# The last stage of an audio tower kernel with another layout of the output: 64 consecutive tokens on each partition, weights stacked high over low, two products a mix, and the output sums shared with GpSimd

## Chip, cores and metric

The kernel runs on one core of a Trainium2 chip. The metric is device time in microseconds (us) of one execution, lower is better. TensorE is called PE in the profile's rows, VectorE DVE, ScalarE ACT, GpSimd POOL, SyncE SP.

## What is computed

The input x is 64 sequences of 125 steps with 128 features. Three parts follow one another:

```python
h = _L0_tok_ref(x, L0_tok_kernel)                      # window-3 convolution to 3x128, tanh / sigmoid gates, recurrence over t
h = h + _L0_attn_ref(_layernorm(h), A, B, h0)           # long convolution per channel, gelu
h = h + _L0_ffn_ref(_layernorm(h), gate_weight, w1, w2) # 16 experts, top 2 per token
```

The last part is what matters here. Every one of the 64 x 123 = 7872 tokens picks 2 of 16 experts; each expert's hidden vectors are averaged over its tokens, and one output vector per expert is made of the mean. A token's result is a mix of two of the 16 output vectors:

```python
h = silu(einsum('td,efd->tef', x, w1))
h_sum = einsum('tef,te->ef', h, mask); h_mean = h_sum / max(counts, 1)
y_mean = einsum('ef,edf->ed', h_mean, w2)
out = einsum('tk,tkd->td', routing_w, y_mean[top_idx])
```

## The kernel before

The residual H lies in SBUF as 123 partitions (t) by 64 sequences (b) by 128 features. `build` writes one instruction stream per engine (`@block.sync` for SP, `@block.gpsimd`, `@block.tensor`, `@block.scalar`, `@block.vector`), ordered by hand; semaphores join them, and each engine runs its own stream in order.

**The expert stage.** GpSimd gathers 138 tiles of 128 tokens from the DRAM array `table` (`gather`, L613-617), 3 to a group. The first 60 tiles have places of their own in XN; from then on 24 places (8 groups) are used in turn, and GpSimd waits for TensorE's `group_mm` before it overwrites a group (L624). For each group TensorE transposes 3 tiles (L899), ScalarE copies them out (L1248), then TensorE multiplies each with its expert's w1 (L929), ScalarE does silu in PSUM (L1259) and VectorE adds the tile to the expert's sum (L1706). Six PSUM banks go round, so TensorE waits for the add of tile n-6. 60 tiles are written out, 72 are a loop, 6 are written out again (L1039-1047). On SP the load of w2 stands behind a wait for TensorE's 20th group (L522-523).

**The picks' matrix.** At tiles 16 and 17 VectorE makes L, 123 x 64 x 16: for each token the weights of its two picks at their experts' places (L1782, L1784), and sets `R_ready`. It is needed transposed, with 8 sequences x 16 experts = 128 rows. This is done in two rounds, at tiles 23 and 26 (`RT_AT`): TensorE makes 4 transposes into bank P[5] (L1019), ScalarE rounds them to the high part (L1272), VectorE subtracts for the low part (L1791).

**The end.** Expert sums go through a product with ones (L1056, or as high and low part L1062 and L1063 with a cast by ScalarE, L1325, and a subtraction by GpSimd, L637), and VectorE reduces each over w2 (L1807) to y. Two transposes (L1067) bring y in rows; ScalarE copies it 8 times under the mask `bmask`, one sequence's 16 rows each (L1330), and VectorE makes the 8 low parts (L1815). Then come 16 mixes of 4 sequences: three products each (high x high, low x high, high x low, L1081) in one of 4 banks, an add into H by VectorE (L1822), and a store of H to `out` (L437), the even ones by SP, the odd by ScalarE. Such a store has 123 x 4 pieces of 512 bytes, since tokens of one t and neighbouring b lie 123 x 128 numbers apart in `out`. Every store is cut into 112 partitions and 11 (`SPLIT`).

## Time and profile before

| | |
|---|---|
| median of 3 runs | 514.2 us (513.64 to 516.24) |
| the profiled execution | 512.89 us |
| its span in the trace | 511.1 us |
| busy, share of the span | PE 78%, DVE 61%, ACT 43%, POOL 40% |
| DMA | 43.68 MB in 53020 packets, 85 GB/s on the mean |
| TensorE's granted clock | 0.867 of full speed |

The profile is of one execution. Engine shares are means over stages with different limits, so they do not name the bound of any one stage; the stretches and timelines in the section on rows do. "PEld" is TensorE's loading of weights. In rows of a timeline the bracket at the end gives the engine's idle time before the instruction and what ended it; "issue" there means that it waited for nothing that the profile shows.

### The profile page before, as it was taken

The numbers are of one execution on the slowest core, as the hardware profiler recorded it, in microseconds if no ns is written. First come the engines' busy times: TensorE is split into PE (matmuls) and PEld (weight loads), VectorE is DVE, ScalarE is ACT, GpSimd is POOL, SyncE is SP. The second block draws the span as 40 slices with busy tenths as digits, with TensorE's granted clock in tenths as the row PEclk, the third lists the DMA queues.
The fourth block names the chain that finished last, engine by engine and source line by source line (L and its number), as shares of the span: only waits on it lengthen the run. The fifth ranks groups of instructions, "written<-read, shape, count | busy, mean of one in ns | idle before, by whom it ended". The sixth has DMA issues, their size and how long they took to land.

```text
span 511.1 us, 7309 instructions
## 1 busy us (share of the span) xinstructions
PE 399.0 (78%) x1929; PEld 268.5 (53%) x1930; DVE 311.2 (61%) x827; ACT 217.9 (43%) x423; POOL 205.0 (40%) x231
## 2 busy tenths in 40 slices
PE   8999999998998987240458414589979796899983
PEld 7888888887998964120344101244434242344562
DVE  3598888889788999600354111477744453467894
ACT  3334555554233766320536101456644463457320
POOL 2011101116202998776055776400066665610510
PEclk9999999998998996755668756699997987989997
DMA  7207433322219330922341122100191111100039
GB/s 180 64 1 183 127 101 87 90 79 81 80 34 292 85 80 14 291 52 51 126 153 43 53 53 55 26 5 2 50 327 46 47 41 41 46 10 1 1 78 240
DMA packets 53020, 43.68 MB, mean 85 GB/s; under 512 B 20686, under 2 KB 45980, under 8 KB 52732
## 3 DMA queue, kind: packets, MB, share of 16 engines
q1 hardware_dynamic: 44276, 32.09, 21.9%
q0 software_dynamic: 4416, 9.05, 6.7%
q10 hardware_dynamic: 4296, 2.15, 1.6%
q8 instruction: 15, 0.25, 0.2%
q14 instruction: 17, 0.14, 0.1%
HBM read 34.86 MB, written 8.42 MB: 85 GB/s over the span
## 4 chain that ended last, share of the span: by engine, by line
PE 47%; another core or an unknown queue 16%; DVE 15%; ACT 8%; issue 7%; POOL 3%; DVEq 2%; ACTq 0%; POOLq 0%
PE P L656 18%; PE P L929 13%; PE P L861 5%; ACT P L1259 4%; DVE BIG L1706 3%; DVE H L1822 2%; PE P L899 2%; PE P L1056 2%; PE P L649 2%; PE P L682 1%; POOL XN L597 1%; ACT XN L1180 1%; DVE arena L1498 1%; POOL arena L594 1%
## 5 line engine op out<-in xcount | busy, mean ns | idle before, releaser
L929 PE MATMUL P<-w1T,arena 128*128 x276 | 144.8, 657 | 23.3 <-DVE BIG L1706 14.9
L1706 DVE TENSOR_TENSOR BIG<-BIG,P 128x512 f32 x138 | 94.9, 688 | 103.9 <-issue 57.9
L929 PEld LDWEIGHTS P<-w1T,arena 128*128 128x128 f32 x276 | 51.7, 208 | 79.1 <-issue 78.7
L614 POOL DMA_INDIRECT XN<-table,arena x60 | 58.0, 967 | 39.2 <-issue 18.5
L1259 ACT ACTIVATE P<-P 128x512 f32<-128x512 f32 x138 | 72.8, 580 | 1.6 <-PE P L929 1.5
L1248 ACT COPY arena<-P 128x384 f32<-128x384 f32 (+1 forms) x48 | 22.4, 466 | 110.6 <-remote 63.3
L614 POOL DMA_INDIRECT arena<-table,arena x42 | 39.6, 944 | 60.9 <-PE P L929 44.1
L557 POOL TENSOR_TENSOR rs<-ve,mhalf 123x4 f32<-123x4 f32 x16 | 17.5, 1096 | 101.9 <-DVE ve L1350 101.9
L1097 ACT ACTIVATE arena<-P 128x492 f32<-128x492 f32 x48 | 27.9, 583 | 50.4 <-PE P L656 50.4
L614 POOL DMA_INDIRECT BIG<-table,arena x36 | 34.5, 958 | 22.3 <-remote 10.4
L656 PE MATMUL P<-xh,wh 128*128 128x498 f32 x144 | 42.3, 402 | 0.0
L656 PE MATMUL P<-xh,wl 128*128 128x498 f32 x144 | 40.5, 390 | 0.0
L656 PE MATMUL P<-xl,wh 128*128 128x498 f32 x144 | 40.4, 389 | 0.0
L656 PEld LDWEIGHTS P<-xl,wh 128*128 128x128 f32 x144 | 27.2, 189 | 5.6
L656 PEld LDWEIGHTS P<-xh,wl 128*128 128x128 f32 x144 | 27.1, 188 | 5.4
L861 PE MATMUL P<-XN,BIG 123*123 123x112 f32 (+1 forms) x256 | 27.7, 271 | 1.2 <-DVE XN L1395 1.2
L656 PEld LDWEIGHTS P<-xh,wh 128*128 128x128 f32 x144 | 26.2, 192 | 4.1
L861 PEld LDWEIGHTS P<-XN,BIG 123*123 123x123 f32 x256 | 27.6, 188 | 1.4 <-DVE XN L1395 1.4
L594 POOL TENSOR_TENSOR arena<-arena,mhalf 123x16 f32<-123x16 f32 x4 | 11.7, 2925 | 31.6 <-DVE arena L1514 31.6
L899 PE MATMUL P<-ident,XN 128*128 128x128 f32 x60 | 11.0, 296 | 16.7 <-issue 10.1
L597 POOL TENSOR_SCALAR XN<-H,arena 123x128 f32<-123x128 f32 x24 | 23.3, 985 | 0.3
L899 PEld LDWEIGHTS P<-ident,XN 128*128 128x128 f32 x60 | 8.0, 152 | 27.4 <-issue 27.4
(242 smaller groups left out, 637.9 us busy)
## 6 DMA issues: line engine op xcount, KB each, us to landing
arena<-kpad SPq DMA_DIRECT2D x16, 492.0 KB, 4.0
XN<-in_L_ffn_w SPq DMA_DIRECT2D x1, 4096.0 KB
arena<-in_x SPq DMA_DIRECT2D x16, 224.0 KB
table<-XN SPq DMA_DIRECT2D x4, 896.0 KB
BIG<-table SPq DMA_DIRECT2D x1, 2048.0 KB
out<-H SPq DMA_DIRECT2D x8, 224.0 KB
out<-H ACTq DMA_DIRECT2D x8, 224.0 KB
BIG<-table SPq DMA_DIRECT2D x1, 1024.0 KB
```

Of the source, the lines that this page charges most:

```text
L557: nc.gpsimd.tensor_tensor(rs1[0:T, k], ve1[0:T, k], mhalf[0:T, 0:CB], ALU.pow).then_inc(rstd1, 1)
L594: nc.gpsimd.tensor_tensor(rs2[0:T, qb], ve2[0:T, qb], mhalf[0:T], ALU.pow).then_inc(rstd2, 1)
L597: a = nc.gpsimd.tensor_scalar(XN[0:T, b], H[0:T, b], mm2[0:T, 0, b:b + 1], rs2[0:T, b:b + 1], ALU.subtract, ALU.mult)
L614: pool.indirect_dma_start(out=row_of(n), out_offset=None, in_=table[0:(QA * QB + 1) * TROW, :] if n < NA else table[:, :], in_offset=bass. ...
L656: mm = nc.tensor.matmul(PG[g][:, 0:NV], wpart[:, w, g * D:(g + 1) * D], xpart[:, k, w:w + NV], start=(place == 0 and w == 0), stop=(place ...
L861: mm = nc.tensor.matmul(PG[g % 3][0:T, j * B:j * B + n], hank[0:T, c // HP % HRES, c % HP], XF[0:T, c * B:c * B + n], start=True, stop=True)
L899: mm = nc.tensor.transpose(PT[:, j * SLOT:(j + 1) * SLOT], src, ident[:])
L929: mm = nc.tensor.matmul(bank[:, :], stat, w1T[:, bass.ds(e * FF, FF)], start=True, stop=True)
L1097: nc.scalar.activation(dst[:, k].rearrange("p (b t) -> p b t", b=CB), src, func).then_inc(gate_act, 1)
L1248: nc.scalar.copy(GTs[:, bank, 0:count * SLOT], PT[:, 0:count * SLOT]).then_inc(GT_ready, 1)
L1259: nc.scalar.activation(bank[:, :], bank[:, :], ACT.Silu).then_inc(silu_done, 1)
L1706: v.tensor_tensor(at, at, bank[:, :], ALU.add).then_inc(esum_step, 1)
```

## The change

1. **Layout of the last stage.** After the norms have read H for the last time, SP writes H to `out` as it is (512-byte pieces) and reads it back so that partition p holds the 64 consecutive tokens 64p to 64p+63 (4 KB pieces). At the end a store of 4 tokens per partition is one piece of 2 KB (`ov`).
2. **The picks' matrix takes the same trip.** L goes to `out` in pieces of 64 bytes and comes back twice in pieces of 256 bytes, side by side (`twice`): 4 tokens x 16 experts, and the same 64 numbers again.
3. **Transposes of it.** 4 rounds in place of 2. Rounds 0 and 1 stand among the last six tiles, rounds 2 and 3 behind them; nothing is left at tiles 23 and 26. A transposed tile has the weights in rows 0 to 63 and again in 64 to 127; ScalarE rounds all 128 rows, VectorE makes the low part in rows 64 to 127 alone.
4. **Two products a mix.** (high over low) x high of y with 128 rows, and high x low of y with 64 rows. y is copied for 4 tokens in place of 8; GpSimd folds `bmask` for it at the start. The mixes have 6 banks in place of 4.
5. **Sums.** Of the 16 sums GpSimd makes numbers 2, 5, 8, 11, 14, each after a copy from PSUM by ScalarE; VectorE makes the other 11.
6. 3 warming products in place of 8 stand before the expert sums' products.

```diff
@@ layout, names, sharing
+        twice = R2.rearrange("p k b e -> p (k b e)").rearrange("p (n m) -> p n m", n=NCH)
-        RTh, RTl = (a[:, :, 0:4 * T].rearrange("p h (g t) -> p h g t", g=4) for a in (xh, xl))
-        yh, yl = (a[:].rearrange("p w n -> p (w n)")[:, 0:HB * D].rearrange("p (b d) -> p b d", b=HB) for a in (wh, wl))
+        RT = [a[:, h, 0:4 * T] for a in (xh, xl) for h in range(2)]
+        yh, yl = (a[:].rearrange("p w n -> p (w n)")[:, 0:CB * D].rearrange("p (b d) -> p b d", b=CB) for a in (wh, wl))
-        PRT = P[5]
+        PRT = (P[5], P[5], P[5], P[4])
+        MIX = (P[0], P[1], P[2], P[3], P[6], P[7])
-        RT_AT = (23, 26)
+        RT_ROUNDS = 4
+        ADD_POOL = list(range(2, 2 * NHB, 3))
+        ADD_DVE = [n for n in range(2 * NHB) if n not in ADD_POOL]
-        ov = out.rearrange("b t d -> t b d")
+        ov = out.rearrange("b t d -> (b t d)").rearrange("(p r d) -> p r d", p=T, r=B)
@@ SP
             clear(15, 6, 8)
+            by_t = out.rearrange("b t d -> t b d")
+            for g in range(NQ):
+                for lo, hi in ((0, SPLIT), (SPLIT, T)):
+                    sp.dma_start(by_t[lo:hi, g * QB:(g + 1) * QB], H[lo:hi, g * QB:(g + 1) * QB]).then_inc(H_out, 16)
+            sp.wait_ge(H_out, 2 * NQ * 16)
+            for r in range(0, B, HB):
+                for lo, hi in ((0, SPLIT), (SPLIT, T)):
+                    sp.dma_start(H[lo:hi, r:r + HB], ov[lo:hi, r:r + HB]).then_inc(H_in, 16)
+            sp.wait_ge(H_in, 2 * NHB * 16)
+            sp.wait_ge(R_ready, 1)
+            sp.dma_start(bass.AP(out.tensor, 0, [[E, T], [T * E, B], [1, E]]), L[0:T]).then_inc(R_out, 16)
+            sp.wait_ge(R_out, 16)
+            for k in range(2):
+                sp.dma_start(twice.rearrange("p n (k m) -> p n k m", k=2)[0:T, :, k],
+                             bass.AP(out.tensor, 0, [[B * E, T], [CB * E, NCH], [1, CB * E]])).then_inc(R_in, 16)
             sp.wait_ge(group_mm, EARLY_GROUPS)
@@ GpSimd
+            nc.gpsimd.tensor_tensor(bmask[:, 0:CB], bmask[:, 0:CB], bmask[:, CB:HB], ALU.add)
...
+            pool.wait_ge(H_in, 2 * NHB * 16)
+            for i, n in enumerate(ADD_POOL):
+                pool.wait_ge(mix_copied, i + 1)
+                hv = H[0:T, 4 * n:4 * (n + 1)].rearrange("p b c -> p (b c)")
+                nc.gpsimd.tensor_tensor(hv, junk[i % 2][0:T], hv, ALU.add).then_inc(mixed_pool, 1)
@@ TensorE
+            def weights(h):
+
+                if h == 0:
+                    pe.wait_ge(R_in, 32)
+                elif h < 3:
+                    pe.wait_ge(RT_low, h)
+                for k in range(4):
+                    mm = nc.tensor.transpose(PRT[h][:, k * T:(k + 1) * T], twice[0:T, 4 * h + k], ident[0:T, 0:T])
+                mm.then_inc(RT_mm, 1)
...
-            keep_warm(PT, 8)
+            weights(2)
+            weights(3)
+            pe.wait_ge(esum_step, NT - REGS + 1)
+            keep_warm(P[0], 3)
...
             for n in range(2 * NHB):
...
+                at = slice(n % 4 * T, (n % 4 + 1) * T)
+                nc.tensor.matmul(MIX[n % len(MIX)][0:T, :], RT[n // 4][:, at], yh.rearrange("p b d -> p (b d)"),
+                                 start=True, stop=False)
+                if n == 0:
+                    pe.wait_ge(yl_ready, 1)
+                nc.tensor.matmul(MIX[n % len(MIX)][0:T, :], RT[n // 4][0:64, at], yl[0:64].rearrange("p b d -> p (b d)"),
+                                 start=False, stop=True).then_inc(mix_mm, 1)
@@ ScalarE
+            def high_weights(h):
+                act.wait_ge(RT_mm, h + 1)
+                nc.scalar.copy(RT[h], PRT[h][:, 0:4 * T]).then_inc(RT_high, 1)
...
+                if n in (NT - REGS, NT - REGS + 2):
+                    high_weights((n - NT + REGS) // 2)
+            high_weights(2)
+            high_weights(3)
...
+            stores = list(range(1, 2 * NHB, 2))
+            for i, n in enumerate(ADD_POOL):
+                act.wait_ge(mix_mm, n + 1)
+                if i >= 2:
+                    act.wait_ge(mixed_pool, i - 1)
+                nc.scalar.copy(junk[i % 2][0:T], MIX[n % len(MIX)][0:T, :]).then_inc(mix_copied, 1)
+                store(act, stores[i])
+            for n in stores[len(ADD_POOL):]:
                 store(act, n)
@@ VectorE
+            def low_weights(h):
+                dve.wait_ge(RT_high, h + 1)
+                low = RT[h][64:128]
+                v.tensor_tensor(low, PRT[h][64:128, 0:4 * T], low.bitcast(FP32), ALU.subtract).then_inc(RT_low, 1)
+
             for n in range(NT - REGS, NT):
                 add_tile(n)
+                if n in (NT - REGS, NT - REGS + 2):
+                    low_weights((n - NT + REGS) // 2)
+            low_weights(2)
+            low_weights(3)
...
+            dve.wait_ge(H_in, 2 * NHB * 16)
+            for n in ADD_DVE:
                 dve.wait_ge(mix_mm, n + 1)
```

The order on TensorE at the last six tiles, before. `P<-w1T,arena` is a tile's product, `P<-ident,arena 128x128` the transpose of the next tile:

```order
L899 MATMUL P<-ident,arena 128x128
L929 REGISTER_ALU x2
L929 ISA
L929 MATMUL P<-w1T,arena 128x512
L929 REGISTER_ALU x2
L929 ISA
L929 MATMUL P<-w1T,arena 128x512
L899 MATMUL P<-ident,arena 128x128
L929 REGISTER_ALU x2
L929 ISA
L929 MATMUL P<-w1T,arena 128x512
```

And in the changed kernel, from the same transpose on (L943 is the old L899, L973 the old L929, L1075 are the picks' transposes of `weights`):

```order
L943 MATMUL P<-ident,arena 128x128
L1075 MATMUL P<-ident,arena 128x123 x4
L973 REGISTER_ALU x2
L973 ISA
L973 MATMUL P<-w1T,arena 128x512
L973 REGISTER_ALU x2
L973 ISA
L973 MATMUL P<-w1T,arena 128x512
L943 MATMUL P<-ident,arena 128x128
L1075 MATMUL P<-ident,arena 128x123 x4
L973 REGISTER_ALU x2
L973 ISA
```

Round 0 comes ahead of the second and third of the six tiles, round 1 ahead of the fourth.

ScalarE in the last stage, changed kernel (L1383 is the copy of a mix for GpSimd, L458 a store in its two parts):

```order
L1377 ACTIVATE wh<-P,bmask 128x128 x4
L1383 COPY arena<-P 123x512
L458 DMA out<-H 112x512
L458 DMA out<-H 11x512
L1383 COPY arena<-P 123x512
L458 DMA out<-H 112x512
L458 DMA out<-H 11x512
```

Copies and odd stores alternate five times, then three more stores follow; before, eight masked copies were followed by eight stores.

## Rows read from the trace of the kernel before

**Rows 1.** The page's chain of work that ended last: shares by engine.
```profile
PE 47%; another core or an unknown queue 16%; DVE 15%; ACT 8%; issue 7%; POOL 3%; DVEq 2%; ACTq 0%; POOLq 0%
```

**Rows 2.** Stretches: start:end, length, busy us (count) by engine, clock, DMA share, GB/s.
```profile
core 0: us, PE busy (x) PEld busy (x) DVE busy (x) ACT busy (x) POOL busy (x), PEclk, DMA share, GB/s
283.00:325.00 42.00, 12.55 (x21) 3.74 (x20) 4.81 (x7) 4.58 (x10) 27.28 (x30) 0.59 0.18 46
...
340.00:370.00 30.00, 30.00 (x94) 14.64 (x93) 20.49 (x31) 19.95 (x42) 0.00 (x0) 1.00 0.06 14
370.00:452.00 82.00, 67.48 (x172) 29.68 (x171) 39.83 (x58) 36.99 (x77) 50.02 (x53) 0.88 0.28 89
```

**Rows 3.** Timeline of VectorE at the last tiles and the first reduction.
```profile
471.23 5.61 DVE L1706 TENSOR_TENSOR BIG<-BIG,P 128x512 f32 x7 [0.22 <-DVE BIG L1706]
478.16 0.69 DVE L1807 CUSTOM_DVE_ANT_0 arena<-XN,P 128x512 f32<-128x512 f32 x1 [1.33 <-PE P L1056]
```

**Rows 4.** Timeline, last stage: start, length, instruction, count, idle before and its releaser.
```profile
490.38 2.18 ACT L1330 ACTIVATE wh<-P,bmask 128x128 fp32r<-128x128 f32 x8 [3.80 <-PE P L1067]
490.86 2.16 DVE L1815 SCALAR_TENSOR_TENSOR wl<-P,bmask,wh 128x128 fp32r<-128x128 f32 x8 [1.00 <-ACT wh L1330]
...
492.93 11.13 DVE L1822 TENSOR_TENSOR H<-P,H 123x512 f32<-123x512 f32 x16
...
493.64 13.57 SPq L437 DMA_DIRECT2D out<-H  x16
```

**Rows 5.** Stretches, DMA alone: start:end, length, clock, DMA share, GB/s.
```profile
494.00:509.00 15.00, 0.88 0.99 259
369.00:381.00 12.00, 1.00 1.03 374
...
500.00:502.00 2.00, 1.00 1.04 271
...
508.00:510.00 2.00, 0.50 0.83 227
510.00:512.00 2.00, 0.50 0.01 3
```

**Rows 6.** Groups by line and shape, 476 to 490 us: busy us, mean ns.
```profile
L637 POOL TENSOR_TENSOR wl<-BIG,wh 128x512 fp32r<-128x512 f32 x7 | 8.9, 1278 | 25.9 <-ACT wh L1325 25.8
L1325 ACT CAST wh<-BIG 128x512 fp32r<-128x512 f32 x7 | 4.2, 617 | 7.1 <-PE P L1063 5.5 <-DVE BIG L1706 1.6
```

**Rows 7.** Timeline at tiles 23 and 26: the two rounds of picks' transposes.
```profile
333.73 0.46 PEld L1019 LDWEIGHTS P<-ident,arena 123*128 123x128 f32 x4 [0.56 <-DVE arena L1784]
333.83 0.59 PE L1019 MATMUL P<-ident,arena 123*128 123x123 f32 x4
...
337.05 0.58 ACT L1272 CAST xh<-P 128x492 fp32r<-128x492 f32 x1
...
338.29 0.66 DVE L1791 TENSOR_TENSOR xl<-P,xh 128x492 fp32r<-128x492 f32 x1
...
339.10 0.61 PE L1019 MATMUL P<-ident,arena 123*128 123x123 f32 x4 [1.69 <-DVE xl L1791]
...
339.55 0.49 PE L899 MATMUL P<-ident,XN 128*128 128x128 f32 x3
```

**Rows 8.** Waits of SP's queue: us in total, times, longest us.
```profile
SPq L523 <- PE P L929: 101.8, 1, 101.8
```

**Rows 9.** Timeline of GpSimd: end of the long train of gathers, and the next.
```profile
317.42 0.94 POOL L614 DMA_INDIRECT BIG<-table,arena  x1 [0.31 <-issue]
324.55 0.94 POOL L614 DMA_INDIRECT BIG<-table,arena  x1 [6.19 <-remote]
```

**Rows 10.** DMA issues: queue, count, KB each, median us from issue to landing.
```profile
arena<-kpad SPq DMA_DIRECT2D x16, 492.0 KB, 4.0
...
kpad<-H ACTq DMA_DIRECT2D x1, 128.0 KB, 1.7
```

**Rows 11.** Timeline of TensorE: six passes of three tiles, twice.
```profile
437.75 2.74 PE L929 MATMUL P<-w1T,arena 128*128 x6
...
445.87 4.75 PE L929 MATMUL P<-w1T,arena 128*128 x6
```

More of the change, by code:

```diff
@@ L400, in build @@
         R_ready = sem("R_ready")
+        R_out = sem("R_out")
+        R_in = sem("R_in")
+        H_out = sem("H_out")
+        H_in = sem("H_in")
         RT_mm = sem("RT_mm")
@@ L429, in hankel @@
             return bass.AP(kpad.tensor, q * HP * KROW, [[1, 128], [KROW, HP], [1, T]])
[L431 removed]
+        ov = out.rearrange("b t d -> (b t d)").rearrange("(p r d) -> p r d", p=T, r=B)
         def store(queue, n):
[L435 removed]
+            queue.wait_ge(*added(n))
             for lo, hi in ((0, SPLIT), (SPLIT, T)):
@@ L1008, in _ @@
                 expert_of(n)
-                if n in RT_AT:
-                    pe.wait_ge(R_ready, 1)
-                    h = RT_AT.index(n)
-                    if h == 0:
-                        pe.wait_ge(ring_read, MATCH_AT[NQ - 1, PER_Q - 1] + 1)
-                    else:
-                        pe.wait_ge(RT_low, h)
-                    for k in range(4):
-                        b = (4 * h + k) * HB
-                        mm = nc.tensor.transpose(PRT[:, k * T:(k + 1) * T],
-                                                 L[0:T, b:b + HB].rearrange("p b e -> p (b e)"), ident[0:T, 0:T])
-                    mm.then_inc(RT_mm, 1)
             with pe.Fori(0, PASSES) as i:
@@ L1036, in _ @@
                                group_mm if k == 0 else None)
-            nc.tensor.matmul(PRT[:, 0:128], onef[:], onef[:], start=True, stop=True).then_inc(last_mm, 1)
+            def weights(h):
[6 more added lines that the diff above has]
+                mm.then_inc(RT_mm, 1)
+            nc.tensor.matmul(PRT[0][:, 0:128], onef[:], onef[:], start=True, stop=True).then_inc(last_mm, 1)
             expert_of(NT - REGS)
             transposes_of(TRIPLES + 1)
+            weights(0)
             expert_of(NT - REGS + 1)
@@ L1043, in _ @@
             transposes_of(TRIPLES + 2)
+            weights(1)
             expert_of(NT - 3)
@@ L1328, in _ @@
             act.wait_ge(y_transposed, 1)
-            for b in range(HB):
+            for b in range(CB):
                 nc.scalar.mul(yh[:, b], P[4][:, 0:128], bmask[:, b:b + 1]).then_inc(yh_ready, 1)
-            for n in range(1, 2 * NHB, 2):
+            stores = list(range(1, 2 * NHB, 2))
[6 more added lines that the diff above has]
+            for n in stores[len(ADD_POOL):]:
                 store(act, n)
@@ L1812, in _ @@
             dve.wait_ge(y_transposed, 1)
[L1813 removed]
+            for b in range(CB):
                 dve.wait_ge(yh_ready, b + 1)
[L1815 to L1819 removed]
+                a = v.scalar_tensor_tensor(out=yl[0:64, b], in0=P[5][0:64, 0:128], scalar=bmask[0:64, b:b + 1],
+                                           in1=yh[0:64, b].bitcast(FP32), op0=ALU.mult, op1=ALU.subtract)
+            a.then_inc(yl_ready, 1)
+            dve.wait_ge(H_in, 2 * NHB * 16)
+            for n in ADD_DVE:
                 dve.wait_ge(mix_mm, n + 1)
                 hv = H[0:T, 4 * n:4 * (n + 1)].rearrange("p b c -> p (b c)")
[L1822 removed]
+                v.tensor_tensor(hv, MIX[n % len(MIX)][0:T, :], hv, ALU.add).then_inc(mixed, 1)
 _INS = ["x", "L0_tok_kernel", "L0_attn_A", "L0_attn_B", "L0_attn_h0", "L0_ffn_gate_weight", "L0_ffn_w1", "L0_ffn_w2"]
```

44 lines of the change are left out of this document (13 added, 31 removed).

## The prediction

> **What bounds the kernel now.** I read the shares of the chain first [rows 1]: TensorE has 47% of it, so no single engine is the bound everywhere; the stages must be taken apart. The table by stretches [rows 2] does that: look at how much of a stretch each engine is busy. Two kinds of stretches matter here. From 340 to 370 us TensorE is busy 30.0 of 30 us: anything taken off TensorE in front of it is taken off the end. From 283 to 325 and from 370 to 452 us no engine is full; there GpSimd issues gathers and the others crawl.
>
> The last stretches are the object of the change. From 467 on the adds of the last tiles run back to back on VectorE, 7 of them in 5.61 us, and the first reduction over w2 starts 1.3 us after the last add [rows 3]. At 490.4 the picks' matrix is built, then VectorE makes the 16 output sums in 11.13 us without a gap [rows 4]: TensorE's 48 products do not hold it up. But VectorE is not the end either. It is through at 504.06; the span goes on to 511.1, and there is still DMA at a share of 0.83 from 508 to 510. From the first store on, all DMA engines are full, at 259 GB/s on the mean and 271 in a full stretch [rows 5]. So the end is set by writing 4.03 MB (123 x 64 rows of 512 bytes) in pieces of 512 bytes, from 493.6 (end of the first add) to about 510.2, 16.6 us.
>
> **The tail.** With 64 tokens in a row on a partition, a store of 4 tokens is one piece of 2 KB per partition. No row shows such a write. The nearest on one side is the same write in 512-byte pieces, 259 to 271 GB/s; on the other the load of w2, also 2 KB pieces and also with all engines full, but reading HBM: 374 GB/s with some gathers in it [rows 5]. I take 374, because both cases have a share of 1.0 and differ mainly in bytes per piece. 4.03 MB / 374 GB/s = 10.8 us.
>
> The Trainium skill, in "DMA: Bandwidth & Descriptors", section Specifications, says that 512 bytes is the smallest transfer at line rate, by which 2 KB pieces would write no faster. The trace disagrees as far as reads go [rows 5]; no row shows the write, so this stays a rival, below.
>
> Can the sums feed this? VectorE now makes 11 at 0.69 us = 7.6 us. GpSimd makes 5: a two-input 128x512 operation took it 1278 ns, and ScalarE's copy of 512 columns before each is some 617 ns [rows 6]. Counted from the first product (sum n ready = 0): VectorE's sums 0, 1, 3, 4 are done at 0.7, 1.4, 2.1, 2.8, GpSimd's 2, 5, 8, 11, 14 at about 3.3, 4.6, 5.9, 7.2, 8.5. SP stores the even sums in order, so it holds 4 and 6 behind sum 2; ScalarE stores the odd ones and its later copies queue behind the wait for sum 5 (4.6). Three stores go out early, then the queue idles about 0.5 us until 3.3, and from there the other 13 follow each other at 0.67 us. The end comes at about 13.1, or 12.4 after the first add against 16.6 now: **-4.2 us**.
>
> Ahead of it, ScalarE makes 4 masked copies of y instead of 8 and VectorE 4 low parts instead of 8, 0.27 us each [rows 4]. Eight low parts now end at 493.02, where the first add could start; four end at about 491.95, then comes the second product, so the first add starts at 492.4: **-0.5 us**.
>
> **The weights' transposes, taken out at tiles 23 and 26.** TensorE waited 0.56 us for VectorE's sum of the picks and did four transposes (about 0.45 more until its next work); at tile 26 it sat idle 1.69 us until VectorE, which was behind by the picks' multiplications, had made the low part, then four transposes again [rows 7]. Together 0.56 + 0.45 + 1.69 + 0.45 = 3.15. Without them TensorE runs a little into the wait for its banks, so I take **-2.7 us**; bounds 0 and 3.15. This is in front of the full 30 us of TensorE [rows 2], and the restart of the gathers and w2's load are both tied to TensorE's progress, so what follows should move up with it.
>
> **The same work, put at the end.** Four rounds of four transposes, a cast on ScalarE (0.58 us as at L1272) and a low part on VectorE (0.66 us as at L1791) [rows 7]. Rounds 0 and 1 stand among the last six tiles, where VectorE has no gap. They cost it 2 x 0.66 = 1.3. Round 1 costs more: its transposes reuse round 0's bank and wait for VectorE's low part 0, which comes after the add of tile NT-6; behind that wait in TensorE's order are the last three tiles. Walking it through with the durations of the rows: low part 0 ends at 473.4 (this trace's time scale), transposes to 474.05, tile 135's add at 475.75, the last two tiles' adds at 477.2 and 478.1, the end at 478.8 instead of 476.84: +2.0. Low parts 2 and 3 (1.3 us) fit into the 1.32 us before the first reduction [rows 3]. ScalarE's last two casts end about 0.45 us after the last add and push its first cast of an expert's sum by as much: +0.4. **+2.4 us**, bounds 1.3 (VectorE's work alone) and 3.5.
>
> **The two trips through `out`.** SP writes H (4 MB, 512-byte pieces) and reads it back in 4 KB pieces, from 265 us on. At the rates of [rows 5] that is 15 + 11 us and two latencies, over by about 295. SP has nothing else: its next wait, for w2, lasts 101.8 us [rows 8]. Gathers share the DMA engines, but they are needed 20 us and more later, and GpSimd's pace of one per 1.25 us decides that stage: its train of gathers ends at 317.42 and the next comes at 324.55 [rows 9]. It costs nothing as long as that pace holds. The second trip, of the picks' matrix, starts when R_ready is set (333.7) and must be back when TensorE reaches round 0 of the transposes, at 469.4 - 2.7 = 466.7: 133 us of cover. The extra GpSimd add at the start stands beside TensorE's warm-up: nothing.
>
> **Sum.** -4.2 - 0.5 - 2.7 + 2.4 = -5.0. The profiled execution took 512.9 us (span 511.1), so 507.9 on its scale. It was 1.3 us under the median of the runs (514.2), so the forecast is **509.2 us**, 1.0% faster.
>
> **Rivals.**
>
> *The small pieces come back too late (slower).* R_out has 123 x 64 = 7872 pieces of 64 bytes, R_in 3936 of 256. Spread over 16 engines that is 738 per engine; over three it is 3936. The nearest rows: 1024 pieces of 492 bytes landed in 4.0 us, a 128-piece write in 1.7 [rows 10], so (4.0 - 1.7) / 64 = 36 ns a piece; a full stretch of the 512-byte write gives 30 (512 bytes at a 16th of 271 GB/s) [rows 5]. Sixteen engines need 27 us. Three need 3936 x 36 + 3.4 = 145 us, 12 more than the cover: 521 us. It decides from 33 ns a piece; 64-byte pieces should be cheaper than that. Against 16 engines speaks that each other transfer of 123 rows in this kernel is cut in 112 and 11, and these three are not. 11%.
>
> The same page of the Trainium skill ("Why a DMA increments its semaphore by 16 and not by 1") says that a DMA uses the largest number of engines up to 16 that divides its outermost count; for 123 this is 3. No row here shows it.
>
> *2 KB pieces write no faster than 512-byte ones.* The engines are full in the tail already, and if a piece costs by its bytes the write stays at 16.6 us: -0.5 - 2.7 + 2.4 = -0.8, 513.4 us. Against it stands the 374 of [rows 5]. 8%.
>
> That is what the rule of the Trainium skill's "DMA: Bandwidth & Descriptors" quoted above would give.
>
> *The middle keeps the 2.7 us.* Between 370 and 452 us gather trains and slow stretches follow each other, and TensorE is busy only 67 of 82 us [rows 2]; a stage that waits on itself can swallow a shift. 511.9 us. 14%.
>
> *GpSimd's sums are slow beside VectorE's.* At twice 1278 ns five take 12.8 us, the last store comes near 16: 512.1 us. Against it: the reduction beside L637 takes its 0.69 us at 478.16 as others do [rows 3]. 6%.
>
> *TensorE's clock falls while it waits for round 1 and for the last add.* After an idle stretch at 443 us six passes took 4.75 us instead of 2.74 [rows 11]; twice that price on the sums' products gives +4, 513.2 us. 8%.
>
> **How the numbers follow.** The forecast keeps 53%; its own range is 507.1 (end +1.3, middle -3.15, tail 0.6 better) to 511.5. About 0.5%, 2.6 us, is what a measurement of this kernel can tell from no change: the bounds are 511.6 and 516.8. Faster: the forecast's 53%, half of the middle rival, and 4 of the 22% of the three rivals behind it, whose prices are upper ones: 49 + 7 + 4 = 0.60 (4 of the 53 fall within). Within: 4 + 7 + 14 of the 22 = 0.25. Slower: the late trip, and 4 where two of the others meet: 0.15. The range for 8 in 10 reaches from 505.5 (the forecast's low end, and the scatter of the runs shown, 2.6 us, once more in part) to 515.5, over the rivals but the late trip.
>
> **What would show it.** Last stretch: DMA share 1.0 at 350 GB/s or more, last packet some 12.4 us after the first add; if under 290 GB/s, the tail is wrong. At tiles 23 and 26 no idle time of TensorE. VectorE's last tile add about 2 us later, relative to the last gather, with four 64x492 operations. GpSimd's five sums near 1.3 us. R_in landed before 466. If w2's load or TensorE's first `weights` waits on DMA, the forecast is wrong by that wait.

## The result and the profile after

The changed kernel is slower: 520.38 us (median of 4 runs, 518.10 to 521.75) against 513.92 us. The ratio is 1.0121, 95% interval 1.0086 to 1.0156. The forecast was 509.2 us, 505.5 to 515.5.

The two profiled executions are 519.14 us (span 517.4) and 512.89 us (span 511.1), so there are 6.3 us to explain. The later runs fell on chips of two kinds: on chips 4 and 12 the kernel before takes 512 to 515 us, as in the first measurement; on chips 1 and 2 it takes 421 us. Times are therefore compared as ratios to the kernel before on the same chip.

The page of the changed kernel has this line to set beside [rows 1] (shares by engine of the chain of work that ended last):

```profile
PE 50%; another core or an unknown queue 15%; DVE 11%; ACT 9%; issue 8%; POOL 3%; DVEq 1%; POOLq 0%; ACTq 0%
```

The entry POOLq (GpSimd's queue) has 0%, there as here, and looks like nothing, but here it is the last link. This is the end of the chain of the changed kernel in order of time (start, length, what):

```profile
503.52 0.59 ACT arena L1383
504.12 0.07 issue
504.19 1.30 POOL H L682
505.48 1.20 issue
506.69 1.32 POOLq L140
```

The span ends at 517.4, on GpSimd's queue, and on an instruction of L140, the line of the block that frames the whole program. The record calls it a DRAIN, the instruction with which GpSimd ends its stream; it ends at 517.17, when nothing else runs; the kernel before ended its chain in VectorE's sums. The stretches of the changed kernel say so (columns as in [rows 2]):

```profile
494.00:500.00 6.00, 6.00 (x15) 2.52 (x14) 3.45 (x5) 1.17 (x2) 2.17 (x2) 1.00 0.48 146
500.00:506.00 6.00, 6.00 (x16) 2.57 (x15) 3.46 (x6) 1.17 (x2) 3.00 (x3) 1.00 0.80 259
506.00:512.00 6.00, 0.86 (x3) 0.31 (x2) 0.69 (x1) 0.59 (x1) 1.28 (x1) 0.60 0.82 266
...
513.00:517.00 4.00, 0.00 (x0) 0.00 (x0) 0.00 (x0) 0.00 (x0) 0.00 (x0) 0.50 0.00 0
```

Two things are to be seen. First, four whole microseconds without an engine and without DMA. Second, the DMA share in the tail is 0.48 and 0.80, where it was 0.99 in [rows 5]: the writes no longer set the pace, they wait for sums and, as shown below, for their issue. The timeline shows for whom the sums wait (start, length, instruction, idle time before it and its releaser):

```profile
494.14 0.18 PEld L1123 LDWEIGHTS P<-wh,xh 128*123 128x123 f32 x1 [0.24 <-issue]
494.14 0.49 PE L1123 MATMUL P<-wh,xh 128*123 128x512 f32 x1
494.32 1.46 DVE L1878 TENSOR_TENSOR H<-P,H 123x512 f32<-123x512 f32 x2 [0.65 <-PE P L1127]
494.56 0.18 PEld L1127 LDWEIGHTS P<-wl,xh 64*123 64x123 f32 x1 [0.24 <-issue]
494.56 0.49 PE L1127 MATMUL P<-wl,xh 64*123 64x512 f32 x1
494.97 0.18 PEld L1123 LDWEIGHTS P<-wh,xh 128*123 128x123 f32 x1 [0.24 <-issue]
...
496.77 0.69 DVE L1878 TENSOR_TENSOR H<-P,H 123x512 f32<-123x512 f32 x1 [1.00 <-PE P L1127]
...
506.72 1.28 POOL L682 TENSOR_TENSOR H<-arena,H 123x512 f32<-123x512 f32 x1 [1.24 <-ACT arena L1383]
506.90 0.69 DVE L1878 TENSOR_TENSOR H<-P,H 123x512 f32<-123x512 f32 x1 [0.99 <-PE P L1127]
```

Weight loads start every 0.42 us, and each has 0.24 us of idle time before it. A busy PE (6.00 of 6) hides this: MATMUL spans are drawn so that they touch. In the kernel before the loads of the same stage follow each other every 0.23 us with no idle time:

```profile
495.04 0.18 PEld L1081 LDWEIGHTS P<-wl,xh 128*123 128x123 f32 x1
495.27 0.18 PEld L1081 LDWEIGHTS P<-wh,xh 128*123 128x123 f32 x1
495.50 0.18 PEld L1081 LDWEIGHTS P<-wh,xl 128*123 128x123 f32 x1
```

So 32 products at 0.42 us (13.5 us) replaced 48 at 0.23 us (11.2 us): fewer products, more time. VectorE waits about 1 us for TensorE ahead of five of its eleven sums, those that follow a mix left to GpSimd.

An idle time before a load proves nothing by itself. The tile products of the kernel before have 128 rows each time, and their loads too stand 0.42 us apart with 0.24 us before each:

```profile
434.84 2.74 PE L929 MATMUL P<-w1T,arena 128*128 x6
435.28 0.19 PEld L929 LDWEIGHTS P<-w1T,arena 128*128 128x128 f32 x1 [0.24 <-issue]
435.70 0.19 PEld L929 LDWEIGHTS P<-w1T,arena 128*128 128x128 f32 x1 [0.24 <-issue]
```

Those operands are declared as plain fp32, those of the mixes as fp32r (`xh`, `xl`, `wh`, `wl`), so the comparison that counts is between mixes of the two kernels.

ScalarE holds stores back as well. Its queue has a copy and an odd store in turn, and a store that is ready waits for the copy in front of it:

```profile
503.52 0.58 ACT L1383 COPY arena<-P 123x512 f32<-123x512 f32 x1 [1.95 <-PE P L1127]
503.53 0.79 ACTq L458 DMA_DIRECT2D out<-H  x2
506.07 4.06 ACTq L458 DMA_DIRECT2D out<-H  x8
```

The stores at 503.53 and 506.07 are those of mixes 7 and 9, whose sums ended at 500.84 and 502.52: 2.7 and 3.5 us late. In the run without sums on GpSimd (a1, below) every odd store goes 0.03 to 0.04 us after its sum.

Where the 6.3 us are, from the records of the two traces (start or end in us of the span; the profiles of two experiments beside them):

| | before | changed | a1 | a3 |
|---|---|---|---|---|
| 131st tile add starts | 470.32 | 469.97 | 470.50 | 469.26 |
| last tile add starts | 476.14 | 477.82 | 479.52 | 478.28 |
| first output sum starts | 492.93 | 494.32 | 496.00 | 494.77 |
| last sum ends | 504.06 | 508.00 | 509.29 | 504.43 |
| last packet of a store ends | 510.27 | 512.44 | 512.26 | 510.10 |
| DRAIN of GpSimd (L140) ends | 497.11 | 517.17 | 500.49 | 499.24 |
| span | 511.1 | 517.4 | 513.2 | 511.2 |

Column by column, changed less before: up to the 131st tile -0.35; the last tiles +2.0; expert sums and the low parts of y -0.3; from the first sum to the last packet +0.8; from the last packet to the end +4.1. That makes +6.3. These are single profiles: the 131st tile scatters by 2.2 us between profiles, and in the kernel before the stretch from the first sum to the last packet is 16.8 us in another profile (b1).

### The profile page after: what moved, and what is told of

Same layout as the page of the kernel before. It is cut to its first block, busy times and chain, and to the rows that moved or that the text cites. A ratio compares the mean times of both kernels' runs of the same rounds, so it can differ in the third digit from the quotient of the medians.

```text
span 517.4 us, 7306 instructions
## 1 busy us (share of the span) xinstructions
PE 399.2 (77%) x1911; PEld 265.0 (51%) x1912; DVE 308.9 (60%) x820; ACT 220.7 (43%) x426; POOL 211.5 (41%) x237
## 4 chain that ended last, share of the span: by engine, by line
PE 50%; another core or an unknown queue 15%; DVE 11%; ACT 9%; issue 8%; POOL 3%; DVEq 1%; POOLq 0%; ACTq 0%
PE P L700 15%; PE P L973 14%; PE P L905 6%; ACT P L1303 5%; PE P L943 2%; PE P L735 2%; PE P L1102 2%; DVE BIG L1760 2%; PE P L693 1%; POOL XN L636 1%; ACT XN L1224 1%; DVE arena L1552 1%; PE P L823 1%; POOL arena L633 1%
## 5 line engine op out<-in xcount | busy, mean ns | idle before, releaser
L973 PE MATMUL P<-w1T,arena 128*128 x276 | 144.4, 656 | 15.6 <-DVE BIG L1760 9.5
L973 PEld LDWEIGHTS P<-w1T,arena 128*128 128x128 f32 x276 | 52.7, 210 | 71.9 <-issue 71.7
L943 PE MATMUL P<-ident,XN 128*128 128x128 f32 x60 | 11.1, 299 | 28.0 <-issue 15.0
L905 PE MATMUL P<-XN,BIG 123*123 123x112 f32 (+1 forms) x256 | 29.4, 280 | 2.6 <-DVE XN L1449 2.6
L905 PEld LDWEIGHTS P<-XN,BIG 123*123 123x123 f32 x256 | 29.2, 197 | 2.8 <-DVE XN L1449 2.8
L943 PEld LDWEIGHTS P<-ident,XN 128*128 128x128 f32 x60 | 8.3, 156 | 38.7 <-issue 38.7
```

Of the source, the lines that this page charges most:

```text
L905: mm = nc.tensor.matmul(PG[g % 3][0:T, j * B:j * B + n], hank[0:T, c // HP % HRES, c % HP], XF[0:T, c * B:c * B + n], start=True, stop=True)
L943: mm = nc.tensor.transpose(PT[:, j * SLOT:(j + 1) * SLOT], src, ident[:])
L973: mm = nc.tensor.matmul(bank[:, :], stat, w1T[:, bass.ds(e * FF, FF)], start=True, stop=True)
```

## The experiments

The theory has two parts. A: GpSimd's closing DRAIN lasts a fixed time beyond its last work, and the last sums on GpSimd brought it out from under the stores. B: the change between 128-row and 64-row weights exposes each load. The rivals are named in the expectations.

**1. No sums on GpSimd (a1).** Of the changed kernel:

```diff
-        ADD_POOL = list(range(2, 2 * NHB, 3))
+        ADD_POOL = []
```

> The changed kernel with all 16 last sums on VectorE, none on GpSimd. Theory A: GpSimd ends the program with a DRAIN that lasts 9.2 us beyond its last operation (it ends at 497.1 us in the kernel before, where GpSimd's last work ends at 487.9, and at 517.2 in the changed one, where that ends at 508.0), and this sets the end of the changed kernel. Then it ends near 499 here, and the span ends with SyncE's wait for the last store: 512.3 to 513.3 us instead of 517.4, a time of about 514.5. Rival: the DRAIN only lasts until something else is over (the last stores, the other engines), and the span stays at 517 us. TensorE's products stay at 0.42 us each in both.

Measured: 515.72 us, ratio 1.0003 (0.9969 to 1.0037); span 513.2. The DRAIN ends at 500.49 and the span at the last store. GpSimd's last operation ends at 491.33 here, 9.16 us ahead of that; in the changed kernel it is 508.00 and 517.17. A holds. From the first sum to the last packet it is 16.3 us, where the changed kernel has 18.1: the held stores of ScalarE are gone with the copies. The ratio fell by 0.0118 (6.1 us), the span by 4.2; between their intervals anything from 2.5 us on is open, so the runs ask for no second cause. The products still go at 0.42 us.

**2. 128 rows in both products (a2).** The low weights stand in rows 64 to 127 of RT, so yl over all rows only adds low times low.

```diff
-                nc.tensor.matmul(MIX[n % len(MIX)][0:T, :], RT[n // 4][0:64, at], yl[0:64].rearrange("p b d -> p (b d)"),
+                nc.tensor.matmul(MIX[n % len(MIX)][0:T, :], RT[n // 4][:, at], yl.rearrange("p b d -> p (b d)"),
...
-                a = v.scalar_tensor_tensor(out=yl[0:64, b], in0=P[5][0:64, 0:128], scalar=bmask[0:64, b:b + 1],
-                                           in1=yh[0:64, b].bitcast(FP32), op0=ALU.mult, op1=ALU.subtract)
+                a = v.scalar_tensor_tensor(out=yl[:, b], in0=P[5][:, 0:128], scalar=bmask[:, b:b + 1],
+                                           in1=yh[:, b].bitcast(FP32), op0=ALU.mult, op1=ALU.subtract)
```

> The changed kernel with the second product of each mix over all 128 rows (and yl made for all 128) instead of 64. Theory B: the change between weights of 128 and of 64 rows keeps the next load from running beside the product, so each product costs 0.42 us (load 0.18 + columns 0.23). With 128 rows in both the distance falls to 0.23 us as in the kernel before, the last sum ends near 502.5 instead of 508 us, and GpSimd's DRAIN ends near 512: span 511.8 to 513 us. Rival: two products a bank instead of three, or six banks in turn, cause the 0.42 us: then the distance stays, and the span stays at 517.4 us.

Measured: 516.57 us, ratio 1.0038 (1.0009 to 1.0067); span 515.4. TensorE's loads in its timeline:

```profile
498.24 0.18 PEld L1123 LDWEIGHTS P<-wh,xh 128*123 128x123 f32 x1
498.48 0.18 PEld L1127 LDWEIGHTS P<-wl,xh 128*123 128x123 f32 x1
498.71 0.18 PEld L1123 LDWEIGHTS P<-wh,xh 128*123 128x123 f32 x1
```

0.23 us again, with twice the rows in every second product. B holds for these products, and two products a bank or six banks are not the cause. VectorE makes its 11 sums in one run of 7.57 us. The span is 2.4 us over the 513 expected because the tiles before it were later in this execution (first sum at 496.89); the end of its chain is GpSimd's DRAIN again:

```profile
503.17 1.29 POOL H L682
504.46 0.19 issue
504.66 1.32 POOLq L140
```

**3. Both (a3).** The edits of 1 and 2.

> Both edits at once. If A and B both hold: products every 0.23 us, VectorE bound with 16 sums by 0.69 us (11.1 us, to about 505), the last packet 2 to 3 us later, and a span of 508 to 510.5 us, below the kernel before (511.1). If only A holds: 512.3 to 513.3. If only B: 512 to 513. If neither: 517.4.

Measured: 514.31 us, ratio 1.0006 (0.9979 to 1.0032); span 511.2. Half a miss: both mechanisms are gone, but the span is 0.7 us over the expected upper end and the ratio is not below 1. Its profile is 1.9 us shorter than a1's; by the ratios (1.0006 and 1.0003) the two can't be told apart, so what B costs once A is gone is read from the profiles only: from the first sum to the last packet 15.3 us here, 16.3 in a1. What is left is upstream: the last eight tile adds take 9.0 us (469.26 to 478.28) where they took 5.8.

**4. The kernel before, with late work on GpSimd (b1).** After GpSimd's last subtraction:

```diff
+            pool.wait_ge(mixed, 2 * NHB)
+            nc.gpsimd.memset(junk[0][0:T, 0:4], 0.0)
```

> The kernel before, with one GpSimd memset of 4 columns after the last of VectorE's sums and nothing else. Theory A: the DRAIN runs from about 504.2 us, lasts 9.2 to 10.5 us, and the span grows from 511.1 to 513.6 to 515 us (+2.5 to +4). Rival (the DRAIN ends with the stores): the span stays at 511.1 us.

Measured: 517.44 us, ratio 1.0055 (1.0026 to 1.0084), 2.8 us; span 514.5. The whole difference is one memset of 0.10 us:

```profile
505.04 0.10 POOL L640 MEMSET arena<- 123x4 f32 x1 [16.19 <-DVE H L1824]
```

It ends at 505.14 and the DRAIN at 514.29: 9.15 us. The last packet of a store is through at 510.63, so it is the DRAIN that ends last. This is A in the kernel before, without any of the change.

**5. The order of the products (c4).** The changed kernel with 16 sums on VectorE; the products of two mixes n and n + 1 in turn, first both of 128 rows, then both of 64.

```diff
-            for n in range(2 * NHB):
+            for n in range(0, 2 * NHB, 2):
...
+                for m in (n, n + 1):
+                    at = slice(m % 4 * T, (m % 4 + 1) * T)
+                    nc.tensor.matmul(MIX[m % len(MIX)][0:T, :], RT[m // 4][:, at], yh.rearrange("p b d -> p (b d)"),
+                                     start=True, stop=False)
...
+                for m in (n, n + 1):
+                    at = slice(m % 4 * T, (m % 4 + 1) * T)
+                    nc.tensor.matmul(MIX[m % len(MIX)][0:T, :], RT[m // 4][0:64, at], yl[0:64].rearrange("p b d -> p (b d)"),
+                                     start=False, stop=True).then_inc(mix_mm, 1)
```

> The changed kernel with 16 sums on VectorE (as a1_no_pool), second products over 64 rows, but the products of two mixes grouped: two of 128 rows, then two of 64. Theory B1 (the change of the row count costs): a load that follows a load of the same row count starts 0.23 us after it, one after another count 0.42, 0.65 us a mix on the mean. Theory B2 (a load of 64 rows can't run beside a product at all, and neither can the one behind it): 0.42 us also for the second of two loads of 64 rows, 0.23 only for the second of 128, 0.75 us a mix. If it were the number of products a bank, all stay at 0.42.

Measured in a single execution: 512.75 us; only its loads are used. TensorE's loads, two in a row:

```profile
493.86 0.29 PEld L1125 LDWEIGHTS P<-wh,xh 128*123 128x123 f32 x2 [0.37 <-issue]
494.51 0.29 PEld L1131 LDWEIGHTS P<-wl,xh 64*123 64x123 f32 x2 [0.37 <-issue]
495.17 0.29 PEld L1125 LDWEIGHTS P<-wh,xh 128*123 128x123 f32 x2 [0.37 <-issue]
495.83 0.29 PEld L1131 LDWEIGHTS P<-wl,xh 64*123 64x123 f32 x2 [0.37 <-issue]
```

A pair of either kind takes 0.66 us: two products' columns (0.47) and one load (0.18). So it is the change of the row count (B1, 0.65 a mix expected), and 64 rows by themselves cost nothing (B2 wanted 0.75). The detail expected was wrong: the second load of a pair starts 0.10 us after the first, not 0.23, and runs beside the first product, while at a change the next load starts 0.55 us after the one before it.

The Trainium skill, in "TensorE: Matmul & The Clock Gate", section The mechanism, says that a weight load overlaps with matmuls in flight only when the row group differs; the same section also lets a load into the background weight buffer run ahead. The runs contradict the "only": loads of the same 128 rows overlap in a2, and loads that change from 128 to 64 rows and back do not in the changed kernel. No row shows into which buffer a load goes.

**6. The kernel before without its two rounds (c1).** The transposes of L, casts and subtractions at tiles 23 and 26 are left out, so the mixes read other numbers. (In the code `if n in RT_AT` became `if n in ()` on three engines.)

> The kernel before without its two rounds at tiles 23 and 26 (no transposes of L, no casts to xh and subtractions to xl; the mixes then read other numbers). Theory C: the 2.7 us they cost VectorE are given back behind them, because the stage from 370 to 450 us goes at the pace of GpSimd's gathers and not of VectorE: the 29th tile add (345.0 and 346.4 us in the two profiles of that layout) comes 2 to 2.7 us earlier, but the 131st (470.3 and 471.2) by less than 1 us, and the time falls by less than 1 us. Rival: the gain carries through, and in the changed kernel it was the trips of H and R that ate it: then the 131st add is at 468 us and the time 2.7 us shorter.

Measured on chip 12: 509.85 us, ratio 0.9956 (0.9935 to 0.9976), 2.2 us. The 29th tile add comes at 342.95 and the 131st at 468.21, 2.1 us earlier than in the kernel before (single profiles scatter by as much, so the ratio is the stronger evidence). Theory C falls: in this kernel the gain carries through the gather stage. Then who took it in the changed one?

**7. The trips of H and R alone (f1), beside c1 again.** To c1's kernel the changed kernel's lines on SyncE from `for g in range(NQ)` to R_in were added, with VectorE's waits for H_in and R_in before its sums; the last stores then write other numbers.

> The kernel before without its two rounds (as c1_again), with the changed kernel's trips of H and R through out and back, piece for piece (the stores at the end then put other numbers in other places). Theory D1: the trips share the DMA queues with the gathers and the load of w2 and slow the stage of tiles: the 131st tile add comes 1 to 2 us later than in c1_again (468.2 there), and the ratio is 0.002 to 0.004 above it; this is where the gain of the removed rounds went in the changed kernel. Rival D2: the trips are hidden; 131st add and ratio are those of c1_again within 0.002, and the later tile adds of the changed kernel are scatter between runs.

> c1_before_no_rounds once more, to stand beside f1_trips on the same chip: ratio 0.993 to 0.998.

These ran on chip 1, and two repeats on chips 1 and 2:

> The kernel before without its two rounds, again. If the kernel before takes 512 to 515 us on this chip: ratio 0.9956 as on the second chip, 131st tile add near 468 us. If it takes 421: ratio 1.000.

> The kernel before without its rounds and with the trips of H and R. D1 (the trips slow the gather stage): ratio 0.002 to 0.004 above c1_third's, 131st add 1 to 2 us later. D2 (hidden): ratios within 0.002, as on the fast chip (1.0004 beside 1.0005).

> The kernel before without its two rounds, a last time. On a chip with 512 to 515 us for the kernel before: ratio 0.9935 to 0.998. On one with 421: 1.000.

> The same with the trips of H and R. D1: ratio 0.002 to 0.004 above c1_last's on a chip of the first kind. D2: within 0.002 of it on either kind.

| ratio to the kernel before | first | second | third (chip 2) |
|---|---|---|---|
| without rounds | 1.0005 (0.9988 to 1.0022) | 1.0001 (0.9990 to 1.0013) | 1.0009 (0.9990 to 1.0028) |
| and with the trips | 1.0004 (0.9993 to 1.0015) | 1.0008 (0.9988 to 1.0028) | 0.9999 (0.9982 to 1.0016) |

On these chips the trips cost nothing (D2). They do delay the stage, and it recovers: the 111th tile add comes at 357.2, 356.9 and 356.0 with them and at 355.1, 354.3 and 355.2 without; at the 131st all six lie between 378.5 and 379.5. The first tile add already comes 1.4 to 2.0 us later with them (244.4 to 244.7 against 242.7 to 243.1). But here the rounds cost nothing either (the first of the three missed its 0.993 to 0.998), so the question of chips 4 and 12, where c1 gives 2.2 us, was not answered by these pairs: all fell on the other kind. On the kind of chips 4 and 12 the 131st add comes at 470.32 and 471.23 in the two profiles with the rounds, at 468.21 in the one without, and in the seven profiles with the changed kernel's middle between 469.22 and 471.38, 469.99 on the mean. Experiment 8 adds to this.

**8. No rounds at the end (c2).** a3 without the four rounds (transposes, casts, subtractions; the mixes read other numbers).

> The kernel with both edits (16 sums on VectorE, 128 rows in both products), and without the four rounds at the end (no transposes, casts and subtractions; the mixes then read other numbers; R's trip stays). Theory: the rounds cost what the last eight tile adds take longer (9.0 us from the 131st to the last, 5.8 in the kernel before), so the distance falls to 5.8 us and the time by 2.5 to 3.5 us against a3_both (514.3), to about 511.3. Rival: they are hidden but for the last add's delay of VectorE's own 0.67 us each that lies before it (1.3 us), and the time falls by 1.3 or less.

Measured on chip 12: 509.98 us, ratio 0.9946 (0.9925 to 0.9966). The last seven adds stand in one row again, as in [rows 3]:

```profile
470.52 5.60 DVE L1752 TENSOR_TENSOR BIG<-BIG,P 128x512 f32 x7 [0.22 <-DVE BIG L1752]
477.45 0.69 DVE L1851 CUSTOM_DVE_ANT_0 arena<-XN,P 128x512 f32<-128x512 f32 x1 [1.33 <-PE P L1099]
```

From the 131st to the last add it is 5.8 us, as expected, and the ratio is 0.6% (3.1 us) below a3's, which was measured on chip 4. In a3 the same place reads:

```profile
471.71 0.67 DVE L1849 TENSOR_TENSOR xh<-P,xh 64x492 fp32r<-64x492 f32 x1
472.42 1.51 DVE L1760 TENSOR_TENSOR BIG<-BIG,P 128x512 f32 x2
473.95 0.67 DVE L1849 TENSOR_TENSOR xh<-P,xh 64x492 fp32r<-64x492 f32 x1
474.89 0.69 DVE L1760 TENSOR_TENSOR BIG<-BIG,P 128x512 f32 x1 [0.27 <-ACT P L1303]
476.81 0.69 DVE L1760 TENSOR_TENSOR BIG<-BIG,P 128x512 f32 x1 [1.23 <-ACT P L1303]
478.28 0.69 DVE L1760 TENSOR_TENSOR BIG<-BIG,P 128x512 f32 x1 [0.78 <-ACT P L1303]
```

This run also bears on the question of experiment 7. It ran on chip 12 as c1 did, neither makes a round, and c2 has the trips. From the last tile add to the end of the span c2 is 2.5 us shorter (32.9 against 35.4), yet the medians are 509.98 and 509.85 us and the ratios 0.9946 and 0.9956. So some 2 us are lost ahead of the last tile add. The profiles agree: the 131st add comes at 468.21 in c1 and at 469.60, 469.22 and 470.03 in c2, c4 and d1, which have the trips and ran on the same chip. Ahead of that add the two kernels differ by the trips and by one small GpSimd add at the start, so theory D1 is likely for this kind of chip, but not shown: no run has the trips alone there.

**9. Three rounds later (d1).** a3 with rounds 1 and 2 behind the last tile, round 3 beside the expert sums, and banks P5, P5, P4, P6.

```diff
-        PRT = (P[5], P[5], P[5], P[4])
+        PRT = (P[5], P[5], P[4], P[6])
...
             expert_of(NT - 1)
-            weights(2)
-            weights(3)
+            weights(1)
+            weights(2)
             pe.wait_ge(esum_step, NT - REGS + 1)
             keep_warm(P[0], 3)
             pe.wait_ge(esum_step, NT)
+            weights(3)
```

> Both edits of a3_both, and three of the four rounds moved behind the last tile: rounds 1 and 2 between the last tile add and the first reduction (where VectorE waits 1.3 us for TensorE anyway), round 3 beside the expert sums, its subtraction in the 1.0 us in which VectorE waits for the transposes of y; banks P5, P5, P4 and P6. If theory C2 holds (a round between tile adds makes VectorE and TensorE wait for each other), the last eight adds take 6.5 to 7 us instead of 9.0, the stage between stays at 16.5 us, and the time is about 2 us below a3_both: 512 to 512.7, ratio to before 0.995 to 0.998. Rival: the rounds only move, the stage between grows by what the adds give back, and the time stays at 514.3.

> The repaired version: ratio 0.993 to 0.998 on a chip like the first; 6 to 8 us below the changed kernel on either kind.

The copies of ScalarE and the subtractions of VectorE moved along. Measured: 509.83 us, ratio 0.9950 (0.9927 to 0.9973) on chip 12; 419.86 us, ratio 0.9968 (0.9955 to 0.9980) on chip 1. The last eight adds take 6.43 us, and the stage from the last add to the first sum 16.9 (16.5 in a3): 2.6 us gained and 0.4 given back. VectorE's rows:

```profile
472.48 0.67 DVE L1853 TENSOR_TENSOR xh<-P,xh 64x492 fp32r<-64x492 f32 x1
473.19 3.96 DVE L1764 TENSOR_TENSOR BIG<-BIG,P 128x512 f32 x5
477.18 0.67 DVE L1853 TENSOR_TENSOR xh<-P,xh 64x492 fp32r<-64x492 f32 x1
477.77 0.67 DVE L1853 TENSOR_TENSOR xl<-P,xl 64x492 fp32r<-64x492 f32 x1
478.87 0.69 DVE L1867 CUSTOM_DVE_ANT_0 arena<-XN,P 128x512 f32<-128x512 f32 x1 [0.43 <-PE P L1102]
```

This version leaves nothing out and beats both kernels, the one before by 0.3 to 0.5%. Its ratio stands beside c2's 0.9946, which makes no rounds at all; by the profiles the moved rounds still cost 1.0 us (0.6 in the last eight adds, 0.4 behind them), where a3's cost 3.2.

**10. Two sums on GpSimd, early (f3).** d1 with `ADD_POOL = [2, 5]`.

> d1_rounds_later with two of the sixteen sums (numbers 2 and 5) on GpSimd, early enough that its DRAIN (9.2 us beyond its last work, which ends near 497.5) is over by 507 us, before the last store has landed (508.8). If VectorE's pace of 0.69 us a sum holds the stores back, the last packet comes 0.5 to 1 us earlier and the ratio falls from 0.995 to 0.993 to 0.994. If the writes themselves bound the tail, nothing changes. If GpSimd's DRAIN were longer than measured, the span would grow.

Measured on chip 1: 420.68 us, ratio 0.9983 (0.9971 to 0.9995), not below d1's 0.9968 there. From the first sum to the last packet it is 15.4 us (402.98 to 418.40), not less than in d1 (15.4 on chip 12, 15.0 on chip 1). The DRAIN ended at 416.54, under the stores. So GpSimd's help does not bring the DRAIN out when it is early, and it gains nothing: the writes bound the tail, not the sums.

**The changed kernel again.**

> The changed kernel once more, unedited, as the anchor for the others on this chip and with more runs: a ratio of 1.010 to 1.016 to the kernel before, and a span in which GpSimd's DRAIN ends last.

> The changed kernel again: ratio 1.010 to 1.016 on a chip like the first, 1.017 to 1.021 on a fast one, GpSimd's DRAIN last in the span.

Measured on chip 1: ratios 1.0189 (1.0163 to 1.0215), over the 1.010 to 1.016 expected before the kind of chip was known, and 1.0176 (1.0155 to 1.0197). The loss is larger there, 7.4 to 8.0 us; GpSimd's DRAIN ends last in both profiles, at 427.3 in the first, where the last packet is through at 422.5.

## Why the prediction was wrong

*Tail, -4.2.* This step failed. From the first sum to the end of the span the changed kernel takes 4.9 us more, where the text had 4.2 less: 9.1 us off, in four places.

The largest was in no step at all: GpSimd's DRAIN. GpSimd was treated as free to work to the end since its operations end with the others' (1290 ns each, near the 1278 predicted). But the program does not end with its last operation; GpSimd's stream ends 9.16 us later. In the kernel before this lay under the tail from 487.9 to 497.1 and no view of it showed a row. Price here: 4.1 us.

The second is an order. The text had ScalarE's later copies queue behind other work, but not the odd stores behind the copies. Sharing the sums with GpSimd made the stretch from the first sum to the last packet 18.1 us, against 16.3 without (a1): 1.9 us.

The third: the text fed the sums "counted from the first product" and never priced the products, because in the profile before they did not hold VectorE up. With 64 rows in every second product they cost 0.42 us instead of 0.23, and the sums wait for TensorE: 16.3 us (a1) against 15.3 with 128 rows (a3), 0.9. The second and third act on each other: late products make late copies, and with 128 rows GpSimd's sums cost the stretch only 0.2 us (a2, 15.6).

The first two make the sign: with no sums on GpSimd the ratio falls from 1.0121 to 1.0003 (a1). With 128 rows but GpSimd's sums it is 1.0038 (a2), with both edits 1.0006 (a3).

The fourth is a size. 2 KB pieces do write faster than 512-byte ones, but the 374 GB/s of the read was too high. The stretches of a3 and a2, DMA columns last:

```profile
500.00:505.00 5.00, 1.63 (x7) 0.85 (x6) 4.43 (x8) 0.00 (x0) 0.00 (x0) 0.94 0.96 318
```

```profile
508.00:510.00 2.00, 0.00 (x0) 0.00 (x0) 0.00 (x0) 0.00 (x0) 0.00 (x0) 0.50 1.00 326
```

A full share moves 326 GB/s, against 271 before [rows 5]. A piece takes 97.6 ns on the mean in a3 and 30.6 ns before, all pieces together, divided by the 16 engines, 12.0 against 15.1 us: -3.1, where -4.2 was said. Of that, 2.0 arrives (17.35 us in the profile before, 15.34 in a3), which leaves 2.2 of the 9.1; the start is not full, since the stores come one sum at a time (share 0.68 from 495 to 500 in a3). The text's own sum for the tail also has 1.0 us without a source: 3.3 and 13 times 0.67 make 12.0, not 13.1. It may be the delay from a sum's end to its store's first packet, 0.9 us in the kernel before. This also settles the rival by the Trainium skill ("DMA: Bandwidth & Descriptors", Specifications: 512 bytes is the smallest transfer at line rate): these writes gained 20% in rate from 512 bytes to 2 KB.

*y's masked copies, -0.5, with the +0.4 of the casts.* -0.3 together in the profiles (16.79 to 16.50 us from the last tile add to the first sum), -0.1 said. Near enough.

*Rounds out of tiles 23 and 26, -2.7.* Right as a local price: from the 20th to the 29th tile add it is 10.6 us in the kernel before and 8.3 to 8.4 in c1 and in the changed kernel, -2.2 to -2.3. c1 carries 2.2 us to the end on chip 12. In the changed kernel the waits of 0.56 and 1.69 us of [rows 7] are gone, but its first tile add comes 2.3 us later and its 20th 1.4 later than before. One wait just there is TensorE's, for ScalarE's copy of a gathered group:

```profile
335.30 0.52 PE L943 MATMUL P<-ident,XN 128*128 128x128 f32 x3 [0.86 <-ACT arena L1292]
```

Its 29th add is 0.8 us earlier, its 131st 0.35. That is the rival "the middle keeps it" (14%) in its result; its reason as put there, a stage that swallows a shift, was not confirmed by c1. c2 beside c1 points to the trips (next but one). On chips 1 and 2 the term is nothing.

*Rounds at the end, +2.4 (2.0 of it ahead of the last add).* +2.0 in the profiles of the changed kernel and c4, 3.2 in a1, a2 and a3, 3.1 by the ratios of a3 and c2: within the bounds given (1.3 to 3.5). Why one order of work gives two values was not looked into. The walk-through of round 1, bank and low part 0 in front of three tiles, is what the rows show; in d1, without most of it, the rounds cost 1.0.

*Trips of H and R, 0.* On the kind of chips 1 and 2 right in the end: the first tile add is late by 1.4 to 2.0 us, the 131st is not. On the other kind this term is likely wrong by some 2 us (c2 beside c1), and with it "it costs nothing" failed there. H's trip was longer than the 295 said: its last piece is through at 306.3, and the DMA share is 0.98 and 0.99 in the stretches 265 to 285 and 286 to 305. The rival that R comes back too late is out: R_in's last piece is through at 390.0, 79 us before the transposes of round 0 start (468.85). R_out's 7872 pieces took from 335.0 to 365.1, 3.8 ns each over all engines, against the 11 ns (33 on each of three engines) from which that rival decided. (Its 36 ns a piece divides by 64; 1024 pieces less 128 over 16 engines are 56 an engine, which gives 41.) For R_in the rule of the Trainium skill's "DMA: Bandwidth & Descriptors" ("Why a DMA increments its semaphore by 16 and not by 1", three engines for 123 rows) is near what the trace has: its pieces keep 3.3 engines busy on the mean over 22 us. For R_out it is not: 5.5 are busy. No row names the engines, so the rule is neither shown nor refuted; the price was harmless.

*GpSimd's sums slow beside VectorE's:* no, 1290 ns. *Clock:* the granted clock is 1.00 in the stretches from 466 to 506; no.

The range (505.5 to 515.5) failed because all four errors of the tail have the same sign, and no rival had a price for the end of a program beyond its last packet.

## What to carry to other kernels

When work is moved to an engine that was idle at the end, look at what that engine still has to do after its last instruction. Here GpSimd needs 9.16 us, so its last work has to end that long before the last store lands. When such work also takes a copy by the engine that issues stores, look at which store stands behind which copy. Fewer rows or fewer products are no gain by themselves: compare the distance of the weight loads with that of the same kind of product before, not TensorE's busy time, and keep the row count the same from one load to the next, with rows of zeros or of harmless numbers if need be. And a step that must wait for a bank is best put where its engine waits anyway, not between two steps of a full engine.

## What the runs showed of the hardware

- GpSimd's DRAIN ends 9.15 to 9.16 us after its last operation in all twenty profiles, after a sum of 1.28 us as after a memset of 0.10.
- In the mixes' products (fp32r, 512 columns) loads of weights with the same 128 rows start 0.23 us apart; a change from 128 to 64 rows or back exposes the load of 0.18 us. The tile products (fp32, 128 rows) have 0.42 us without any change.
- Writes of 2 KB pieces: 326 GB/s at full share; of 512 bytes: 271.
- The same program takes 514 us on one kind of chip and 421 on the other. Of the gap 34 us lie ahead of the first tile add (276.4 against 242.7 in c1 on chip 1), where the gathers have been running since 201, and 36 between the first and the 20th. From 283 to 325 us of the kernel before VectorE makes 7 tile adds and is idle 37 us, most of it waiting for nothing that the profile shows; on chip 1 (c1) it makes 28 in 30 us, from 255 to 285:

```profile
L1706 DVE TENSOR_TENSOR BIG<-BIG,P 128x512 f32 x7 | 4.8, 687 | 37.1 <-issue 30.1 <-ACT P L1259 7.0
```

```profile
L1705 DVE TENSOR_TENSOR BIG<-BIG,P 128x512 f32 x28 | 19.2, 688 | 8.3 <-ACT P L1258 5.6 <-DVE BIG L1705 0.8
```

The operations themselves take the same 0.69 us. In the records most of VectorE's register instructions between them take 0.70 us in this stretch of the kernel before, and 0.04 to 0.11 on chip 1; from 340 to 370 us, with no gathers, they take as little on the slower chip too. Why was not tried.
